# Context columns from the host's layout, and one value product in each of eight steps, in a Flamingo block

## The chip, the cores and the metric

The kernel runs as one program on one core of a Trainium2 chip. The metric is the device time of one execution in microseconds (us). The kernel before took 1677.72, 1670.6 and 1677.48 us in three runs, a median of 1677.48 us. Its profiled execution took 1674.65 us; the profile's span, from the first to the last instruction, is 1672.8 us of it.

## The reference

64 sequences of 128 rows and 256 columns pass through a gated cross attention and a quantised feed-forward layer. Cut to what matters:

```python
# attention: 16 heads of 64, one context sequence for each sequence of x
q = layernorm(x) @ Wq;  k = ctx @ Wk;  v = ctx @ Wv          # (64, 128, 1024)
dots = einsum('bhid,bhjd->bhij', q, k) / 8                    # causal and key mask
out  = einsum('bhij,bhjd->bhid', softmax(dots), v)
x = x + tanh(g_xattn) * (out @ Wo + bo)
# feed-forward: 16-bit fake quantisation of the activations after every step,
# 4-bit weights with one scale for 32 values (lpbq_dequant)
x = x + tanh(g_ffn) * ffn(layernorm(x), w_gate, w_up, w_down)
```

`lpbq_dequant` divides each block of 32 weights by its largest magnitude over 7, rounds, and multiplies back.

## The kernel before

The program is a chain of stages. The first, `attention` (L76), makes the attention and the second layernorm; four more make the gate products, the up products, the maxima and the down products of the feed-forward layer. The change touches the first stage and the queue of data for it.

**Tiling.** Sequences go in 16 groups of 4 (NB = 4, 512 tokens). A group has 8 steps; step c makes heads 2c and 2c+1 (128 of the 1024 inner columns). Unit u = 8g + c is one such pair of heads in one group. The first and the last group are written out, and the 14 between them are one loop. The text counts groups from 0 to 15 and steps from 0 to 7.

**One step on TensorE (`step`, L929).** Every fp32 product is three passes of rounded halves (high by high, low by high, high by low) for each of two 128-row parts of the contraction. In order: the q product of unit u (6 matmuls of 512 columns, into one of two PSUM banks `proj`), the k product (6), the output product of unit u-4 (12 of 256 columns, into `y`), the value products of this step (6 each), probabilities times values of unit u-3 into `pv` (`times_v`), and the scores of unit u.

**Banks.** All products that go through `proj` are a list of jobs; job i writes bank i mod 2 and waits (`copied`) until the job two places before it in the list is copied out. So a value product shares its bank with the q product of its step, and waits for ScalarE's copy `qT` (L509).

**The values** of a group are 8 products (4 sequences by 2 halves of 512 columns). `V_AT` spreads them: two in step 0, one in each of steps 1 to 6, none in step 7. VectorE copies those of steps 0 to 2 out (L661), ScalarE those of steps 3 to 6 (L528). Heads of the first half are first used by `times_v` in step 3, those of the second half in step 7.

**The inputs of the next group.** x and the context are loaded with rows on partitions, and TensorE turns them (`transpose_in`, L857) through `proj` in step 7: two jobs of four 128x128 transposes for x, two for the context. For each job ScalarE copies the rounded high half (`tx_hi`, `tc_hi`, L476), and VectorE subtracts it for the low half (`tx_lo`, `tc_lo`, L617).

**Around TensorE.** ScalarE's order in a step: `qT`, four exponentials of unit u-1 for one head, `kT` (L498), four for the other, the rounded probabilities `prob_parts` of the first head (L491), the value copy, the high half of the output `o_hi` (L532), `prob_parts` of the second head. VectorE's: mask and maximum of the first head (L636, L638), `o_lo` for unit u-4 (L643), `probT` (L624), mask and maximum of the second head, reciprocals (L630), and pieces of the layernorms that the step number chooses (`residual`, which reads `y`, in step 3). GpSimd scales the probabilities (L422), makes their low half (L427) and one `probT` (L434), the reciprocal roots of the layernorms (L412 in step 3), and `xres` in step 6 (L448). SP's queue turns the fp16 halves of the probabilities by DMA and loads the inputs.

**Feed-forward weights.** They are loaded with one wait in unit 3 (`load_ffn`), and VectorE dequantises them in group 0 and group 15 (table `beside`, L738): maximum, scale and reciprocal (`weight_scales`), integers (`weight_ints`), values (`weight_values`), always at the end of the step that the table names. The halves of Wo are made at the end of steps 0 to 2 of group 0 (`w_low_part`).

Of the kernel before, what the change touches and what calls it, by code (L numbers as in the profile page):

```python
# [29 lines left out]
P = 128  # L30
NB = 4
# [44 lines left out]
def attention(nc, x, ctx, mask, g_xattn, wq, wk, wv, wo, bo, w_ffn, ident, ones, x1_d, xn2_d, w_raw, amax_x, wd, hand):  # L76
# [14 lines left out]
    V_AT = [[0, 1], [2], [3]] + [[NB + n] for n in range(NB)] + [[]]  # L91
# [4 lines left out]
    jobs += [(NC - 1, "t", n) for n in range(2 * KC)]  # L96
    NJ = len(jobs)
    FIRST = 2 * KC
# [13 lines left out]
    with ExitStack() as st:  # L112
# [11 lines left out]
        ctx_in = sb("ctx_in", [P, NB, D])  # L124
# [65 lines left out]
        high_done = sem("high_done")  # L190
        scored = sem("scored")
# [10 lines left out]
        transposed = sem("transposed")  # L202
# [10 lines left out]
        half_out = sem("half_out")  # L213
# [73 lines left out]
        def _(sp):  # L287
            def load_ctx(g):
                sp.dma_start(ctx_in[:], ctx[bass.ds(g * NB, NB)].rearrange("b p d -> p b d")).then_inc(ctx_loaded, 16)
# [58 lines left out]
            def load_ffn():  # L348
                sp.wait_ge(w_ready, len(PIECES))
                for n, w in enumerate(w_ffn):  # L350
# [9 lines left out]
            for u in range(U):  # L360
# [8 lines left out]
                if u == 3:  # L369
                    load_ffn()  # L370
# [96 lines left out]
        def _(act):  # L467
# [4 lines left out]
            def high(g, i, n):  # L472

                b, before = nth(g, i)
                act.wait_ge(projected[b], before + 1)
                nc.scalar.activation(t_hi[n // KC][:, n % KC, :], proj[b][:], ACT.Copy).then_inc(high_done, 1)  # L476
# [23 lines left out]
            def step(g, c):  # L500
# [23 lines left out]
                if new and c > 2:  # L524
                    for i, n in jobs_of(c, "v"):
                        b, before = nth(g, i)
                        act.wait_ge(projected[b], before + 1)
                        nc.scalar.activation(v_sb[:, n % NB, VH:2 * VH], proj[b][:], ACT.Copy).then_inc(copied[b], 1)  # L528
# [4 lines left out]
                if nxt:  # L533
                    high(g, *ts[3])
                if soft:
                    high_prob(u - 1, 1, c % 2, NC // 2 * g + c // 2)
                if isinstance(g, int) and g == 0 and c < 3:
                    w_high_part(4 + c)
# [3 lines left out]
            for n in range(2 * KC):  # L542
                high(-1, first_job(n), n)
            w_high_part(2)
# [19 lines left out]
            act.wait_ge(transposed, 1)  # L564
# [10 lines left out]
        def _(dve):  # L575
# [37 lines left out]
            def low(g, i, n, high_before):  # L613
# [3 lines left out]
                nc.vector.tensor_tensor(t_lo[n // KC][:, n % KC, :], proj[b][:], t_hi[n // KC][:, n % KC, :].bitcast(F32),  # L617
                                        ALU.subtract).then_inc(copied[b], 1)

# [37 lines left out]
            def values(g, c):  # L657
                for i, n in jobs_of(c, "v"):
                    b, before = nth(g, i)
                    dve.wait_ge(projected[b], before + 1)  # L660
                    nc.vector.tensor_copy(v_sb[:, n % NB, 0:VH], proj[b][:]).then_inc(copied[b], 1)  # L661

            def step(g, c):
# [33 lines left out]
                if c < 3:  # L697
# [7 lines left out]
                if nxt:  # L705
                    for n in range(2, 4):
                        low(g, *ts[n], 2 * KC * (g + 1) + n)
                if isinstance(g, int):
                    for work, n in beside.get((g, c), []):
                        work(n)  # L710
# [9 lines left out]
            def weight_scales(n):  # L720
                dve.wait_ge(ffn_loaded, 48)
                wait(dve, dequantised, 5 * n)
                nc.vector.tensor_reduce(w_max[:], blocks(n), X, ALU.max, apply_absolute_value=True).then_inc(dequantised, 1)
                dve.wait_ge(dequantised, 5 * n + 1)
# [1511 lines left out]
```

## Time and profile before

| | us |
|---|---|
| median of three runs | 1677.48 |
| profiled execution | 1674.65 |
| its span | 1672.8 |
| TensorE matmuls busy | 1558.6 (93%), weight loads 1270.2 (76%) |
| VectorE busy | 1376.2 (82%) |
| ScalarE busy | 1254.1 (75%) |
| GpSimd busy | 1022.8 (61%) |

The span falls into the start (to 13.69 us, where the first q product begins), group 0 (to 91.12), groups 1 to 14 (to 1010.85), group 15 (to 1084.72), the tail of the attention (to about 1110), and the feed-forward stages. Matmuls are pipelined: a busy row of TensorE counts an instruction from its start to its end, though the next has started. How long a part of a step lasts is read from start to start.

### The profile page before, as it was taken

The numbers are of one execution on the slowest core, as the hardware profiler recorded it, in microseconds if no ns is written. First come the engines' busy times: TensorE is split into PE (matmuls) and PEld (weight loads), VectorE is DVE, ScalarE is ACT, GpSimd is POOL, SyncE is SP. The second block draws the span as 40 slices with busy tenths as digits, with TensorE's granted clock in tenths as the row PEclk, the third lists the DMA queues.
The fourth block names the chain that finished last, engine by engine and source line by source line (L and its number), as shares of the span: only waits on it lengthen the run. The fifth ranks groups of instructions, "written<-read, shape, count | busy, mean of one in ns | idle before, by whom it ended". The sixth has DMA issues, their size and how long they took to land. (4 is left out here: it accounts for less than half of the span.)

```text
span 1672.8 us, 38339 instructions
## 1 busy us (share of the span) xinstructions
PE 1558.6 (93%) x12684; PEld 1270.2 (76%) x12684; DVE 1376.2 (82%) x2243; ACT 1254.1 (75%) x3238; POOL 1022.8 (61%) x1004
## 2 busy tenths in 40 slices
PE   7799999999999999999999998889997997995998
PEld 5687877877878778778778786667775776774887
DVE  6778878878888778888788887768887998998997
ACT  5677878778777778787777776747666998985665
POOL 3878878878779788788788796800004665560000
PEclk9999999999999999999999999989998999997999
DMA  5535444544444454445444442439986885664664
GB/s 172 131 78 127 95 101 104 119 101 101 110 106 100 89 126 96 101 104 118 102 101 112 104 100 55 98 118 327 335 286 219 279 282 188 239 245 171 220 220 149
DMA packets 351460, 252.22 MB, mean 151 GB/s; under 512 B 287792, under 2 KB 325808, under 8 KB 348464
## 3 DMA queue, kind: packets, MB, share of 16 engines
q1 hardware_dynamic: 351408, 251.58, 53.3%
q8 instruction: 26, 0.43, 0.1%
q14 instruction: 26, 0.21, 0.0%
HBM read 105.25 MB, written 76.02 MB: 108 GB/s over the span
## 5 line engine op out<-in xcount | busy, mean ns | idle before, releaser
L483 ACT ACTIVATE prob<-masked,neg_max 128x128 f32<-128x128 f32 x1024 | 397.5, 391 | 67.5 <-DVE neg_max L638 65.4
L427 POOL TENSOR_TENSOR prob_parts<-prob,prob_parts 128x512 f16<-128x512 f32 x254 | 299.3, 1197 | 4.2 <-ACT prob_parts L491 2.4
L422 POOL TENSOR_TENSOR prob<-prob,scaled 128x512 f32<-128x512 f32 x256 | 269.8, 1054 | 20.0
L636 DVE TENSOR_TENSOR masked<-score,mask_add 128x512 f32<-128x512 f32 x256 | 174.8, 683 | 70.6 <-PE score L912 70.6
L491 ACT ACTIVATE prob_parts<-prob 128x512 f16<-128x512 f32 x254 | 159.4, 628 | 55.3 <-POOL prob L422 54.0
L483 ACT ACTIVATION_READ_ACCUMULATOR prob<-masked,neg_max 128x1 f32 x1024 | 193.3, 189 | 0.0
L638 DVE TENSOR_REDUCE neg_max<-masked 128x4 f32<-128x512 f32 x256 | 175.6, 686 | 8.8
L434 POOL TENSOR_TENSOR probT<-turn 128x512 f32<-128x512 f16 x125 | 177.7, 1421 | 0.0
L420 POOL TENSOR_TENSOR scaled<-rsums,pscale 128x4 f32<-128x4 f32 x256 | 58.8, 230 | 181.7 <-DVE rsums L630 181.4
L925 PE MATMUL y<-wo_hi,o_hi 128*128 128x256 f32 x508 | 150.3, 296 | 20.1 <-DVE o_lo L643 19.5
L1676 POOL TENSOR_SCALAR xThi<-n_x 128x1024 fp32r<-128x1024 int16 x15 | 44.7, 2981 | 202.4 <-DMA n_x<-n_x_d 166.6
L509 ACT ACTIVATE qT<-proj 128x512 f32<-128x512 f32 x128 | 76.5, 598 | 96.6 <-PE proj L840 96.6
L898 PEld LDWEIGHTS pv<-probT,v_sb 128*64 128x64 f32 x2048 | 110.2, 138 | 46.7 <-issue 43.3
L898 PE MATMUL pv<-probT,v_sb 128*64 128x128 f32 x2048 | 141.6, 281 | 3.7 <-DVE probT L624 2.8
L925 PE MATMUL y<-wo_lo,o_hi 128*128 128x256 f32 x508 | 144.9, 285 | 0.0
L925 PE MATMUL y<-wo_hi,o_lo 128*128 128x256 f32 x508 | 144.6, 285 | 0.0
L1037 PE MATMUL pair<-xThi,wup_hi 128*128 128x512 f32 x312 | 125.0, 401 | 15.6 <-PEq L1397 5.8
L2106 PE MATMUL y<-wd_both,h_hi 128*128 128x512 f32 x384 | 134.6, 394 | 4.7 <-ACT h_lo L2005 4.7
L925 PEld LDWEIGHTS y<-wo_hi,o_hi 128*128 128x128 f32 x508 | 97.3, 191 | 37.4 <-DVE o_lo L643 34.4
L624 DVE TENSOR_TENSOR probT<-turn 128x512 f32<-128x512 f16 x129 | 123.4, 958 | 0.0
L1037 PE MATMUL pair<-xThi,wup_lo 128*128 128x512 f32 x312 | 123.4, 396 | 0.0
L1037 PE MATMUL pair<-xTlo,wup_hi 128*128 128x512 f32 x312 | 123.4, 395 | 0.0
(251 smaller groups left out, 4526.6 us busy)
## 6 DMA issues: line engine op xcount, KB each, us to landing
gate<-gate_d SPq DMA_DIRECT2D x30, 768.0 KB, 4.3
n_x<-n_x_d SPq DMA_DIRECT2D x25, 512.0 KB, 5.1
gate_d<-stage SPq DMA_DIRECT2D x8, 1536.0 KB, 5.5
n_u_d<-w_raw SPq DMA_DIRECT2D x16, 768.0 KB, 4.1
stage<-n_u_d SPq DMA_DIRECT2D x16, 768.0 KB, 6.2
gate_d<-gate SPq DMA_DIRECT2D x7, 1536.0 KB, 5.5
x_in<-in_x SPq DMA_DIRECT2D x16, 512.0 KB, 4.1
ctx_in<-in_ctx SPq DMA_DIRECT2D x16, 512.0 KB, 4.9
```

The lines of the kernel that those rows point to most:

```text
L422: gp.tensor_tensor(prob[:, h], prob[:, h], scaled[:, h, :].rearrange("p (b o) -> p b o", o=1).broadcast_to([P, NB, P]), ALU.mult).then_inc ...
L427: gp.tensor_tensor(prob_parts[:, h, 1], prob[:, h].rearrange("p b k -> p (b k)"), prob_parts[:, h, 0], ALU.subtract).then_inc(prob_low, 1)
L434: gp.tensor_tensor(probT[:, 1], turn[:, slot, 1, 0:NB], turn[:, slot, 1, NB:2 * NB], ALU.add).then_inc(probT_copied[1], 1)
L483: nc.scalar.activation(prob[:, h, b, :], masked[:, h, b, :], ACT.Exp, bias=neg_max[:, h, b:b + 1], accum_out=psums[:, h, b:b + 1]).then_in ...
L491: nc.scalar.activation(prob_parts[:, h, 0], prob[:, h].rearrange("p b k -> p (b k)"), ACT.Copy).then_inc(prob_high, 1)
L624: nc.vector.tensor_tensor(probT[:, h], turn[:, slot, h, 0:NB], turn[:, slot, h, NB:2 * NB], ALU.add).then_inc(probT_copied[h], 1)
L636: nc.vector.tensor_tensor(masked[:, h], score[h][:], mask_add[:], ALU.add).then_inc(masked_done, 1)
L638: nc.vector.tensor_reduce(neg_max[:, h, :], masked[:, h], X, ALU.max, negate=True).then_inc(max_done, 1)
L898: last = nc.tensor.matmul(pv[h * HD:(h + 1) * HD, b, :], v_sb[:, b, c * P + h * HD:c * P + (h + 1) * HD], probT[:, h, b, :], start=True, s ...
L925: last = nc.tensor.matmul(y[:, e, :], o[s][:, e * P:(e + 1) * P], w[m][:, c * D:(c + 1) * D], start=(c == 0 and j == 0 and e % 2 == 0), st ...
L1037: last = nc.tensor.matmul(bank, stat(s, k), mov(m, k), start=(j == 0), stop=(j == len(passes) - 1))
L2106: nc.tensor.matmul(y[b][:, e], h_hi[:, h, cols], wd[:, :, at:at + D], start=(h == 0 and j == 0), stop=(h == 1 and j == HJ - 1), skip_group ...
```

## The change

1. The host hands the context over as columns: `ctx_columns` has 256 rows and 8192 tokens. The kernel loads 256 by 512 of it into `ctx_in`. The two transposing jobs of the context, their two copies on ScalarE and two subtractions on VectorE go. In their place ScalarE rounds the whole tile once (`ctx_high_part`, 128x1024, SBUF to SBUF), and VectorE subtracts once (`ctx_low_part`, 128x1024, both operands in SBUF), after the second x job in step 7. The k product of step 0 waits for it (`ctx_split`); the second half of the q product of step 0 waits for the second x job.
2. `V_AT` has one value product in each step, number n in step n. Those of steps 0, 1, 2 and 7 are copied by VectorE, those of 3 to 6 by ScalarE. TensorE makes the value product right after the k product, in front of the output product. In steps 3 and 7 `times_v` waits for the copy of the value product of the same step.
3. The feed-forward weights are loaded in two parts (down in unit 2, up and gate in unit 4) and dequantised in the order down, gate, up, in smaller pieces and in other steps; some pieces stand in front of the second reciprocals (`between`). The second half of the last weight's values is made in the tail. The low half of Wo is made in two pieces.
4. In group 0 ScalarE rounds the attention weights before the probabilities of the step, not after them.

```diff
-    V_AT = [[0, 1], [2], [3]] + [[NB + n] for n in range(NB)] + [[]]
+    V_AT = [[n] for n in range(NC)]
+    V_DVE = (0, 1, 2, NC - 1)
-    jobs += [(NC - 1, "t", n) for n in range(2 * KC)]
+    jobs += [(NC - 1, "t", n) for n in range(KC)]
...
-                sp.dma_start(ctx_in[:], ctx[bass.ds(g * NB, NB)].rearrange("b p d -> p b d")).then_inc(ctx_loaded, 16)
+                sp.dma_start(ctx_in[:], ctx_t[:, bass.ds(g * T, T)].rearrange("(k p) t -> p k t", p=P)).then_inc(ctx_loaded, 16)
...
-                columns_made(g - 1, 2 * KC - 1)
+                sp.wait_ge(ctx_split, g)
                 load_ctx(g)
...
-                if u == 3:
-                    load_ffn()
+                if u == 2:
+                    load_ffn(5, (2,))
+                if u == 4:
+                    sp.wait_ge(ffn_loaded, 16)
+                    load_ffn(len(PIECES), (0, 1))
...
+            def ctx_high_part(g):
+                act.wait_ge(ctx_loaded, 16 * (g + 1))
+                if not (isinstance(g, int) and g == 0):
+                    (i, _), = jobs_of(NC - 1, "k")
+                    b, before = nth(g - 1, i)
+                    act.wait_ge(projected[b], before + 1)
+                nc.scalar.activation(t_hi[1][:], ctx_in[:], ACT.Copy).then_inc(high_done, 1)
...
                 if soft:
                     exps(u - 1, 0)
-                if nxt:
-                    high(g, *ts[0])
                 if new:
                     copy_k(g, c, u)
                 if nxt:
-                    high(g, *ts[1])
+                    high(g, *ts[0])
                 if soft:
                     exps(u - 1, 1)
                 if nxt:
-                    high(g, *ts[2])
+                    high(g, *ts[1])
+                    ctx_high_part(g + 1)
+                if isinstance(g, int) and g == 0 and c < 3:
+                    w_high_part(4 + c)
                 if soft:
                     high_prob(u - 1, 0, c % 2, NC // 2 * g + c // 2)
-                if new and c > 2:
+                if new and c not in V_DVE:
...
+            def ctx_low_part(g):
+                dve.wait_ge(high_done, (KC + 1) * (g + 1))
+                nc.vector.tensor_tensor(t_lo[1][:], ctx_in[:], t_hi[1][:].bitcast(F32), ALU.subtract).then_inc(ctx_split, 1)
...
+                if c == NC - 1:
+                    values(g, c)
                 if nxt:
-                    for n in range(2):
-                        low(g, *ts[n], 2 * KC * (g + 1) + n)
+                    low(g, *ts[0], (KC + 1) * (g + 1))
+                if isinstance(g, int):
+                    for work, args in between.get((g, c), []):
+                        work(*args)
                 if soft:
                     reciprocals(u - 1, 1)
...
                 if nxt:
-                    for n in range(2, 4):
-                        low(g, *ts[n], 2 * KC * (g + 1) + n)
+                    low(g, *ts[1], (KC + 1) * (g + 1) + 1)
+                    ctx_low_part(g + 1)
...
+            between = {(0, 3): [(w_low_half, (6, 1))],
+                       (0, 4): [(weight_scales, (0,))],
+                       (0, 5): [(weight_values, (0, 0))],
+                       (G - 1, 1): [(weight_max, (1,))],
+                       (G - 1, 2): [(weight_ints, (1,))],
+                       (G - 1, 6): [(weight_max, (2,))],
+                       (G - 1, 7): [(weight_ints, (2,))]}
+            beside = {(0, 0): [(w_low_part, (4,))],
+                      (0, 1): [(w_low_part, (5,))],
+                      (0, 2): [(w_low_half, (6, 0))],
+                      (0, 3): [(weight_max, (0,))],
+                      (0, 4): [(weight_ints, (0,))],
+                      (0, 5): [(weight_values, (0, 1))],
+                      (G - 1, 1): [(weight_scales, (1,))],
+                      (G - 1, 3): [(weight_values, (1, 0))],
+                      (G - 1, 5): [(weight_values, (1, 1))],
+                      (G - 1, 6): [(weight_scales, (2,))]}
...
+                def part_split(k):
+                    if n == 1 and k == 0:
+                        pe.wait_ge(ctx_split, g + 1)
+                    if n == 0 and k == 1:
+                        (j, _), = jobs_of(c, "k")
+                        pe.wait_ge(copied[j % 2], nth(g, j)[1])
...
+                if new:
+                    for i, n in jobs_of(c, "v"):
+                        value(g, i, n)
                 if nxt:
                     transpose_in(g, *ts[0])
                 if oldest:
...
                     out_product(u - 4, (c - 4) % NC)
                 if nxt:
                     transpose_in(g, *ts[1])
-                if first or fourth:
-                    pe.wait_ge(w_ready, 3 if first else 6)
+                if old and c in (3, NC - 1):
+                    (i, _), = jobs_of(c, "v")
+                    b, before = nth(g, i)
+                    pe.wait_ge(copied[b], before + 1)
+                if old:
+                    times_v(u - 3, co, (g, c, u) if new else None)
```

## Rows read from the trace of the kernel before

**Rows 1.** Stretches: engines' busy time, then granted clock, DMA share, GB/s.
```profile
13.69:91.12 77.43, 62.02 (x544) 48.91 (x544) 55.55 (x86) 50.64 (x159) 48.41 (x49) 0.91 0.44 112
91.12:1010.85 919.73, 898.71 (x8961) 729.57 (x8961) 747.00 (x1498) 719.91 (x2465) 762.44 (x827) 1.00 0.46 105
1010.85:1084.72 73.87, 64.92 (x624) 52.61 (x624) 57.43 (x98) 49.77 (x174) 54.90 (x59) 0.95 0.37 80
...
1110.00:1672.80 562.80, 504.99 (x2332) 413.64 (x2332) 490.99 (x502) 419.37 (x407) 147.56 (x50) 0.95 0.70 240
```

**Rows 2.** Waits of TensorE from 0 to 1110 us: total, times, longest.
```profile
PE y L925 <- DVE o_lo L643: 19.5, 21, 3.4
PE proj L840 <- DVE tc_lo L617: 8.9, 16, 1.0
...
PE proj L840 <- ACT v_sb L528: 4.6, 15, 1.3
```

**Rows 3.** Timeline of TensorE, step 3 of group 8: start, duration, instruction.
```profile
575.92 0.50 PE L840 MATMUL proj<-tx_hi,wq_hi 128*128 128x512 f32 x1
...
580.22 0.40 PE L840 MATMUL proj<-wv_hi,tc_hi 128*128 128x512 f32 x1
...
581.70 1.09 PE L898 MATMUL pv<-probT,v_sb 128*64 128x128 f32 x16
...
583.55 0.50 PE L840 MATMUL proj<-tx_hi,wq_hi 128*128 128x512 f32 x1
```

**Rows 4.** Timeline of ScalarE, the value copy of that step.
```profile
582.79 0.58 ACT L528 ACTIVATE v_sb<-proj 128x512 f32<-128x512 f32 x1
```

**Rows 5.** Timeline of TensorE, step 7 of group 8 and step 0 of group 9.
```profile
606.74 0.50 PE L840 MATMUL proj<-tx_hi,wq_hi 128*128 128x512 f32 x1
...
608.63 0.50 PE L840 MATMUL proj<-tc_hi,wk_hi 128*128 128x512 f32 x1 [0.23 <-ACT v_sb L528]
...
612.62 0.65 PE L869 MATMUL proj<-ident,x_in 128*128 128x128 f32 x4 [0.40 <-ACT kT L498]
...
614.68 0.66 PE L869 MATMUL proj<-ident,ctx_in 128*128 128x128 f32 x4
...
616.70 0.50 PE L840 MATMUL proj<-tx_hi,wq_hi 128*128 128x512 f32 x1 [0.53 <-DVE tc_lo L617]
...
626.35 0.50 PE L840 MATMUL proj<-tx_hi,wq_hi 128*128 128x512 f32 x1
```

**Rows 6.** Timeline of ScalarE, the same step 7.
```profile
609.47 0.60 ACT L509 ACTIVATE qT<-proj 128x512 f32<-128x512 f32 x1
...
611.50 0.58 ACT L476 ACTIVATE tx_hi<-proj 128x512 fp32r<-128x512 f32 x1
...
614.95 0.39 ACT L483 ACTIVATE prob<-masked,neg_max 128x128 f32<-128x128 f32 x1
```

**Rows 7.** Timeline of GpSimd, the same step 7.
```profile
616.00 1.04 POOL L422 TENSOR_TENSOR prob<-prob,scaled 128x512 f32<-128x512 f32 x1
617.00 2.29 POOL L427 TENSOR_TENSOR prob_parts<-prob,prob_parts 128x512 f16<-128x512 f32 x2
```

**Rows 8.** Timelines: rounding and subtracting 128x1024 of a weight in SBUF.
```profile
13.25 1.05 ACT L470 ACTIVATE wv_hi<-v_sb 128x1024 fp32r<-128x1024 f32 x1
...
14.34 1.23 DVE L578 TENSOR_TENSOR wv_lo<-v_sb,wv_hi 128x1024 fp32r<-128x1024 f32 x1 [0.19 <-ACT wv_hi L470]
...
30.86 1.67 DVE L578 TENSOR_TENSOR wv_lo<-v_sb,wv_hi 128x1024 fp32r<-128x1024 f32 x1 [2.47 <-ACT wv_hi L470]
```

**Rows 9.** Timeline of TensorE, two long waits for `o_lo`, in groups 0 and 15.
```profile
84.12 0.58 PE L925 MATMUL y<-wo_hi,o_hi 128*128 128x256 f32 x1 [3.09 <-DVE o_lo L643]
...
1048.16 0.39 PE L925 MATMUL y<-wo_hi,o_hi 128*128 128x256 f32 x1 [3.11 <-DVE o_lo L643]
```

**Rows 10.** Stretches of the granted clock (the column before the DMA share) behind these waits.
```profile
84.30:87.50 3.20, 3.20 (x16) 3.20 (x17) 2.31 (x5) 1.80 (x7) 1.24 (x2) 0.52 0.00 0
...
1046.80:1050.20 3.40, 2.04 (x15) 1.96 (x16) 3.35 (x7) 2.27 (x10) 0.41 (x2) 1.00 0.32 53
```

More of the change, by code:

```diff
@@ L73, in __init__, with attention @@
         self.x_transposed = sem("x_transposed")
-def attention(nc, x, ctx, mask, g_xattn, wq, wk, wv, wo, bo, w_ffn, ident, ones, x1_d, xn2_d, w_raw, amax_x, wd, hand):
+def attention(nc, x, ctx_t, mask, g_xattn, wq, wk, wv, wo, bo, w_ffn, ident, ones, x1_d, xn2_d, w_raw, amax_x, wd, hand):
     B, S, D = x.shape
@@ L346, in load_xres, with load_ffn @@
                 sp.dma_start(xres[:], x[bass.ds(g * NB, NB)].rearrange("b p d -> p b d")).then_inc(xres_loaded, 16)
[L348 to L350 removed]
+            def load_ffn(ready, weights):
+                sp.wait_ge(w_ready, ready)
+                for n in weights:
+                    w = w_ffn[n]
                     sp.dma_start(w_raw[:, n * W1:(n + 1) * W1].rearrange("p (c n) -> p c n", n=w.shape[1]),
@@ new lines, in weight_values @@
+            def weight_values(m, half):
+                dve.wait_ge(dequantised, 5 * m + 4)
+                rows = slice(half * NBLK // 2, (half + 1) * NBLK // 2)
+                last = nc.vector.tensor_tensor(blocks(ORDER[m])[:, rows], ints[:, rows], wide(w_scale)[:, rows], ALU.mult)
+                if half == 1:
+                    last.then_inc(dequantised, 1)
+            between = {(0, 3): [(w_low_half, (6, 1))],
[5 more added lines that the diff above has]
+                       (G - 1, 7): [(weight_ints, (2,))]}
@@ L784, in _ @@
             w_low_part(1)
-            for n in range(2 * KC):
+            for n in range(KC):
                 low(-1, first_job(n), n, n)
+            ctx_low_part(0)
             w_low_part(2)
@@ L833, in _, with product @@
             pe.wait_ge(consts, 1)
-            def product(b, before, stat, mov, n=KC):
+            def product(b, before, stat, mov, new_part=None):
                 wait(pe, copied[b], before)
-                passes = [(k, s, m) for k in range(n) for s, m in split(0, 1)]
+                passes = [(k, s, m) for k in range(KC) for s, m in split(0, 1)]
                 for j, (k, s, m) in enumerate(passes):
+                    if new_part is not None and (s, m) == (0, 0):
+                        new_part(k)
                     last = nc.tensor.matmul(proj[b][:], stat(s, k), mov(m, k), start=(j == 0), stop=(j == len(passes) - 1))
@@ L955, in step @@
                     transpose_in(g, *ts[1])
-                if first or fourth:
-                    pe.wait_ge(w_ready, 3 if first else 6)
-                if new:
-                    for i, n in jobs_of(c, "v"):
-                        value(g, i, n)
-                if nxt:
-                    transpose_in(g, *ts[2])
-                if old:
-                    times_v(u - 3, co, (g, c, u) if new and not nxt else None)
-                if nxt:
-                    transpose_in(g, *ts[3], (g, c, u))
-                if new:
-                    if not (nxt or old):
+                if old and c in (3, NC - 1):
[4 more added lines that the diff above has]
+                    times_v(u - 3, co, (g, c, u) if new else None)
+                if new:
+                    if not old:
                         scores_free(g, c, u)
@@ L973, in _ @@
                 nc.tensor.transpose(trans[:, n % NB, :], ident[:], ident[:])
-            for n in range(2 * KC):
+            for n in range(KC):
                 transpose_in(-1, first_job(n), n)
@@ L2160, in program @@
         hand = Handover(nc, before_n_p, G, D, KC, IC)
-        attention(nc, x, ctx, mask, g_xattn, wq, wk, wv, wo, bo, (w_up, w_gate, w_down), ident, ones, x1_d, xn2_d, w_raw, amax_x, wd, hand)
+        attention(nc, x, ctx_t, mask, g_xattn, wq, wk, wv, wo, bo, (w_up, w_gate, w_down), ident, ones, x1_d, xn2_d, w_raw, amax_x, wd, hand)
         gate = sb("gate", [P, N])
```

107 lines of the change are left out of this document (52 added, 55 removed).

## The prediction, made before the result was known

> **What bounds the kernel now.** I read the busy line first, then the span cut into stages, TensorE's waits, and the timeline of one group. The stages: groups 1 to 14 take 919.73 us, with matmuls on TensorE for 898.71 of them at a granted clock of 1.00; groups 0 and 15 take 77.43 and 73.87 us for the same eight steps at 0.91 and 0.95 [rows 1]. A group in the loop is 919.73 / 14 = 65.7 us. The feed-forward part (562.80 us) isn't touched. So three things count: the group in the loop, fourteen times; the two irregular groups; what TensorE waits for.
>
> A step in the middle of a group is full of matmuls: from 575.92 to 583.55, 7.63 us, with a value product of 1.48 us in it (580.22 to 581.70) [rows 3]. Eight of them are 61.0 us, so a group loses 4.7 us elsewhere. The step starts of group 8 and 9 say where: step 7 takes 9.96 us (606.74 to 616.70), step 0 takes 9.65 (616.70 to 626.35) [rows 5], step 5 takes 7.93, the rest 7.63. In steps 7 and 0 stand four transposing jobs of about 0.5 us and two value products instead of one, and waits: for `v_sb`, `kT` and `tc_lo` [rows 5]. The waits of TensorE up to 1110 us are led by `o_lo`, 19.5 us in 21 places, the longest 3.4, then `tc_lo` with 8.9 in 16 [rows 2]. The `o_lo` waits are VectorE being late, the long ones behind pieces of weight work in groups 0 and 15, each about 3.1 [rows 9].
>
> **Steps 7 and 0 in the loop.** I lay the new order over the old starts, in us from the start of step 7 (606.74). The q product is unchanged, the k product starts at 1.89, when ScalarE has copied the value product of step 6 [rows 5]; GpSimd's `xres` is behind that, and it stays. The value product follows at 3.38: its bank needs `qT`, which ends at 609.47 + 0.60, or 3.33 [rows 6]. It ends at 4.80. The first x job needs `kT`. ScalarE now makes `kT` where `tx_hi` stood, at 611.50 or 4.76 [rows 6], so the job starts at 5.40, 0.6 after TensorE is free. It takes 0.41, the output product 1.43, the second x job 0.49, `pv` 1.05, the scores 0.83 (the same parts from start to start in the old step): step 7 ends at 9.61, against 9.96.
>
> In step 0 the q product ends at 11.1 and the k product then waits for the context split. From the last exponential of the second head (old: 614.95) ScalarE needs 0.87 for it and the second x copy, and 1.05 for the new rounding [rows 6, 8]; VectorE starts the subtraction 1.95 after that exponential starts. The new exponential starts at about 7.73, so the subtraction starts at 9.68, takes 1.23 [rows 8], and ends at 10.9 to 11.0: just in time. After that nothing in step 0 waits. The output product starts 4.3 after the start of the step instead of 3.4, while `o_lo` is ready 3.4 after it. Step 0 becomes 7.63 like the others. Together 17.24 against 19.61: 2.37 saved. Step 5 loses its small `o_lo` wait: 0.30 saved.
>
> **The wait that the change adds in step 3.** `times_v` of step 3 now needs the value product of step 3, and ScalarE copies it at 582.79 to 583.37 [rows 4], 7.45 after the start of the step; it stands behind eight exponentials and the rounded probabilities, which wait for GpSimd (the layernorm root is in front of its scaling in this step). The product itself moves 1.4 earlier, the copy does not, since it isn't the product that it waits for. `pv` started at 581.70, 5.78 in [rows 3]; now at 7.50. That is 1.72 us of TensorE standing still in each group. The copy lies at 7.42 to 7.45 in all 14 groups. Queued behind it on ScalarE are `o_hi` and the second `prob_parts`; behind `pv` are the scores, and so the masks of step 4: all move with TensorE and cost nothing more. VectorE's `residual` in the same step waits for the output product, now 1.4 later, inside that gap. In step 7 the same wait is on VectorE's copy, ready near 5.8 against `pv` at 7.73: nothing.
>
> Sum for a group: 2.37 + 0.30 - 1.72 = 0.95 saved; times 14 = 13.3 us. The transposes and products removed from the busy time are worth more (about 2 times 0.5 us of jobs); most of the rest of the 4.7 us was waiting, and 1.7 of waiting comes back in another step.
>
> **Group 0 and the start.** The first q product starts at 13.69 [rows 1]; before it, two x jobs and two context jobs go through two banks with their copies, and only the context pair is dropped: 2.2 us earlier. Steps 0 to 3 are led by the attention weights (rounded by ScalarE, subtracted by VectorE); I lay them out in the new order and get step 3 at about 32.4 (was 37.6). There the new wait bites harder: the copy of that value product stands behind exponentials that wait for the mask and maximum, which wait for the first half of Wo's low part. `pv` starts at about 43.4 (was 46.66), 5 us after TensorE is free, at the lower clock. Step 4 starts 3.3 us earlier than before. Steps 4 to 7 took 7.65, 12.16, 7.62 and 13.56. The 12.16 and the 13.56 are a wait for `o_lo` of 2.9 and 3.09 [rows 9] and a stretch at the lower clock behind it, 3.20 us at 0.52 [rows 10]. In pieces, and with `o_lo` needed 1.4 later, they become about 7.7 and 9.7: 8.4 saved. Together 11.7. Bounds: 8 (step 4 no earlier than before, the rest gone), and 14 (no loss in step 3).
>
> **Group 15.** 73.87 us [rows 1]. Step 1 took 13.90 (`o_lo` 3.35 late, then 6.6 us at the lower clock), step 3 10.99 (3.11 late [rows 9], clock unchanged [rows 10]), step 7 8.82. The pieces now are the maximum in step 1 (about 1.7), integers in step 2 (2.2) and halves of the values (0.9), all behind the output product's need. I take 7.63 for steps 0 to 2 and 4 to 6, 10.0 for step 3 (its copy comes later still, VectorE being loaded), 8.1 for step 7 with its value product: 63.9, or 10.0 saved. Bounds: 6 and 11.5.
>
> **The tail.** Half of the last weight's values (0.9) now stands between the last-but-one `o_lo` and the copy of `probT` that the last `pv` needs; TensorE has the output product for most of it: +0.3, between 0 and +1.5. Loads: the same 512 KB a group, in runs of 2 KB instead of 1 KB, issued a whole group ahead; nothing either way. SP now waits for the split, done 1.4 into step 0, before it loads the next context; behind that wait stand the probability transposes, and it used to reach this point 4.2 into step 0: nothing.
>
> **The clock.** All of groups 1 to 14 ran at 1.00 [rows 1]. A wait of 3.09 was followed by 0.52, one of 3.11 by 1.00 [rows 9, 10]; waits up to 1.4 never lowered it, one of 2.13 in the tail did. The new wait of 1.72 lies between. A fall costs half of some 3.2 us, 1.6 us. From none of the 16 to all 16 groups that is 0 to 26 us. Nearest to it are waits of 1.4 (no fall) and 2.1 (fall), so I take a fall in one group of ten or so: +2.
>
> **The sum.** -13.3 - 11.7 - 10.0 + 0.3 + 2 = -32.7 us. The profiled execution of 1674.65 becomes 1642; it lies 2.8 below the median of the three runs, and the timed value is then 1677.5 - 32.7 = 1644.8, or 1642 if it is near the profiled one. I say 1643.
>
> **Rivals.**
> *A, the context split is late.* VectorE's subtraction has both operands in SBUF. The same instruction took 1.23 when GpSimd was idle and 1.67 when GpSimd was in an operation (29.18 to 31.46) at its start [rows 8]. In step 7 GpSimd scales for 1.04 and goes on to two subtractions of 1.16 (616.00, 617.00) [rows 7], 1.05 and 2.05 after the last exponential; VectorE arrives at 1.95. If it gets its turn at 2.09, it is in time; if the next GpSimd operation is in first, it starts 1.1 later, and the k product of step 0 waits 1.05, fifteen times: +16, so 1659. For it: a margin of 0.1 us. Against: two neighbouring cases where VectorE, arriving in one GpSimd operation, ran before the next.
> The Trainium skill (SBUF — State Buffer, section "SBUF: two separate sides") says that a VectorE operation with two SBUF inputs and a GpSimd operation that reads SBUF exclude each other for the whole instruction, and that the first to start holds the ports. By that rule the case turns on which starts first, and it would give this rival's time if GpSimd is.
>
> *B, the clock falls behind the new wait in nearly every group.* +26 - 2 = +24: 1667. For: the wait is longer than any in the loop now. Against: it is below every wait that was followed by a fall.
>
> *C, the wait in step 3 outweighs the rest: slower.* The mechanism is that of step 3, ScalarE's copy behind GpSimd. It must cost 32.7 / 16 = 2.0 us a group more than my 1.72. That happens if the gap brings a fall of the clock that lasts two stretches (3.2 us) in each group: +51 - 2, so 1692; it decides from 2.0 a group. Against: after `pv` everything is dense again, and single falls lasted one stretch in five of six cases in the attention.
>
> *D, the pieces still delay TensorE in groups 0 and 15*, as before: VectorE is 72 and 78% busy there [rows 1]. Then only the loop and the start pay: 13.3 + 3, so 1661.
>
> **Chances.** Forecast 0.55 (own range 1634 to 1652), A 0.2, B 0.08, C 0.04, D 0.13. Range for 8 in 10: 1633 to 1664. A measurement of this kernel tells 0.5%, 8.4 us, from no change. Faster by more: the forecast, A, D and half of B, 0.9; within 0.5%: 0.06; slower: 0.04.
>
> **What would show it.** In the changed kernel's loop: a `pv` in step 3 with about 1.7 us idle before it, released by ScalarE's `v_sb`; step 3 of 9.35, step 7 of 9.6, step 0 of 7.63 (8.7 if A), step 5 of 7.63, group about 64.7. No `o_lo` wait over 1 us in groups 0 and 15 apart from the tail. A longer `pv` wait in step 3 of groups 0 (about 5) and 15 (about 2.4). The clock of groups 1 to 14 at 0.97 or more. I am wrong if `pv` in step 3 waits for nothing, if value products wait for `qT`, or if step 0 still takes 9 us.

## The result, and the profile after

| | before | after |
|---|---|---|
| median (11 runs each) | 1675.62 us | 1667.36 us |
| lowest to highest | 1670.6 to 1678.67 | 1663.54 to 1669.37 |
| profiled execution, its span | 1674.65, 1672.8 | 1667.13, 1665.3 |

The ratio is 0.9951, 95% interval 0.9939 to 0.9963: 8 us faster, clear of the noise, where 33 were forecast, and outside the range of 1633 to 1664.

The same stretches as [rows 1] in the kernel after (the granted clock is the column before the DMA share). Group 0 begins at 11.61 us, group 1 at 82.49, group 15 at 1013.27; the last row is the rest of the span:

```profile
11.61:82.49 70.88, 58.46 (x537) 45.73 (x537) 55.01 (x89) 50.99 (x159) 47.86 (x49) 0.93 0.51 135
82.49:1013.27 930.78, 885.11 (x8852) 741.73 (x8849) 768.59 (x1485) 719.07 (x2451) 776.77 (x827) 0.99 0.45 104
1013.27:1079.80 66.53, 63.23 (x628) 52.85 (x624) 57.14 (x98) 49.20 (x172) 56.67 (x57) 0.97 0.41 88
1079.80:1665.30 585.50, 523.38 (x2500) 430.00 (x2496) 511.15 (x541) 429.83 (x437) 156.56 (x60) 0.96 0.68 234
```

Start and group 0 gained 8.6 us, group 15 gained 7.3, what follows 2.6 (588.1 before). Groups 1 to 14 became 11.05 us slower, 930.78 against 919.73, though TensorE has 13.6 us less of matmuls in them: removed work turned into waiting. Waits of TensorE from 0 to 1110 us (total, times, longest), against [rows 2]:

```profile
PE pv L952 <- ACT v_sb L543: 37.3, 16, 5.6
PE proj L890 <- ACT v_sb L543: 12.5, 16, 1.0
PE proj L923 <- ACT kT L512: 5.5, 15, 0.5
...
PE y L979 <- DVE o_lo L669: 3.3, 2, 2.2
```

`o_lo` fell from 19.5 to 3.3 and `tc_lo` is gone; in their place `pv` waits 37.3 us for ScalarE's copy of the values, once in each group, in step 3. The step lengths of groups 1 to 14 (start of a q product to the next, mean):

| step | 0 | 1, 2 | 3 | 4 | 5 | 6 | 7 | group |
|---|---|---|---|---|---|---|---|---|
| before | 9.66 | 7.63 | 7.63 | 7.63 | 7.93 | 7.63 | 9.97 | 65.7 |
| forecast | 7.63 | 7.63 | 9.35 | 7.63 | 7.63 | 7.63 | 9.61 | 64.75 |
| after | 7.60 | 7.61 | 10.14 | 8.04 | 7.61 | 7.62 | 10.27 | 66.5 |

Step 3 of group 8 on TensorE, against [rows 3], and ScalarE's copy in it, against [rows 4]:

```profile
571.26 0.50 PE L890 MATMUL proj<-tx_hi,wq_hi 128*128 128x512 f32 x1
...
579.22 1.09 PE L952 MATMUL pv<-probT,v_sb 128*64 128x128 f32 x16 [2.13 <-ACT v_sb L543]
...
581.08 0.50 PE L890 MATMUL proj<-tx_hi,wq_hi 128*128 128x512 f32 x1
```

```profile
578.59 0.58 ACT L543 ACTIVATE v_sb<-proj 128x512 f32<-128x512 f32 x1
```

The copy ends 7.91 us into the step, not 7.45, and `pv` starts at 7.96 instead of 5.78: 2.2 us of waiting. The wait of step 3 is counted here from start to start, as the forecast did: how much later `pv` starts than it would with no wait. That gives 2.19 as the mean of the loop; the idle time in brackets, from the modelled end of the last matmul, is smaller (2.09 to 2.13). Why the copy is later stands two engines up. VectorE's `probT` of this step in the kernel after, and GpSimd's work beside it:

```profile
573.42 1.30 DVE L650 TENSOR_TENSOR probT<-turn 128x512 f32<-128x512 f16 x1
...
575.35 0.69 DVE L664 TENSOR_REDUCE neg_max<-masked 128x4 f32<-128x512 f32 x1
```

```profile
571.87 2.30 POOL L432 TENSOR_TENSOR prob_parts<-prob,prob_parts 128x512 f16<-128x512 f32 x2
```

The same two in the kernel before, for step 3 from 575.92:

```profile
578.08 0.83 DVE L624 TENSOR_TENSOR probT<-turn 128x512 f32<-128x512 f16 x1
```

```profile
576.07 2.30 POOL L427 TENSOR_TENSOR prob_parts<-prob,prob_parts 128x512 f16<-128x512 f32 x2
```

GpSimd's `prob_parts` of the step before starts 0.61 us into step 3, where it started 0.15 in; `probT`, which ends 0.55 after the end of it in both kernels, takes 1.30 instead of 0.83; the maximum, the exponentials and the copy are 0.46 later. So GpSimd's lag behind TensorE is what to follow. It stands for a ring of three engines: GpSimd's scaling waits in turn for VectorE's reciprocals (0.4 to 0.5 us idle in front of it in these steps of the kernel after), and these for ScalarE's exponentials; which of the three leads isn't shown. The end of GpSimd's last `prob_parts` of a step, after the end of that step on TensorE, in group 8:

| step | 0 | 1 | 2 | 3 | 4 |
|---|---|---|---|---|---|
| before | 1.72 | 2.65 | 2.45 | 2.23 | 2.20 |
| after | 3.27 | 3.09 | 2.91 | 1.65 | 2.62 |

At the end of step 7 the lag is 2.60 before and 3.36 after: the long step 0 of before brings it down to 1.72, the short one of after only to 3.27. Of the 1.55 between them 0.44 is left after step 1 (in the kernel before, GpSimd then stands idle 2.04 us for VectorE's reciprocals; in the kernel after 0.46), and it no longer shrinks: 0.46 after step 2.

The clock: first the stretch of step 3 of group 1 up to `pv`, the wait in it, then the stretches behind the same wait in groups 1 and 2 of the kernel after:

```profile
105.30:113.40 8.10, 5.98 (x36) 5.03 (x34) 6.03 (x10) 6.11 (x22) 7.16 (x9) 1.00 0.39 68
114.60:117.90 3.30, 3.30 (x38) 2.74 (x31) 1.88 (x3) 0.90 (x2) 2.94 (x3) 0.54 0.41 79
...
181.50:184.80 3.30, 3.30 (x44) 2.76 (x37) 2.43 (x4) 1.93 (x6) 3.00 (x3) 1.00 0.41 78
```

After the same wait the clock fell to its lower level (1.2 GHz) in groups 1, 3, 5, 7, 10, 12 and 14, and stayed at the upper in the others. Groups with a fall took some 67.1 us, those without 65.9: in steps 3 and 4 together 18.96 against 17.40, in step 7 10.08 against 10.46.

Step 7 of group 8, against [rows 5]:

```profile
603.93 0.50 PE L890 MATMUL proj<-tx_hi,wq_hi 128*128 128x512 f32 x1
...
606.58 0.50 PE L890 MATMUL proj<-tc_hi,wk_hi 128*128 128x512 f32 x1 [0.98 <-ACT v_sb L543]
...
610.08 0.66 PE L923 MATMUL proj<-ident,x_in 128*128 128x128 f32 x4 [0.37 <-ACT kT L512]
...
614.39 0.50 PE L890 MATMUL proj<-tx_hi,wq_hi 128*128 128x512 f32 x1
...
621.99 0.50 PE L890 MATMUL proj<-tx_hi,wq_hi 128*128 128x512 f32 x1
```

The k product starts 2.65 into the step, not 1.89. The bank it needs is freed by the value copy of step 6, behind GpSimd's `xres`, which started 5.25 into step 6 (4.49 before):

```profile
601.55 2.37 POOL L453 TENSOR_TENSOR xres<-xres,bo_g 128x1024 f32<-128x1024 f32 x1
```

```profile
605.41 0.63 ACT L505 ACTIVATE prob_parts<-prob 128x512 f16<-128x512 f32 x1 [2.75 <-POOL prob L427]
605.94 0.58 ACT L543 ACTIVATE v_sb<-proj 128x512 f32<-128x512 f32 x1
```

Step 0 is 7.60: the context split was in time. VectorE was first at it, and GpSimd's pair of subtractions, which started inside it at 614.93, took 2.82 us where the same pair took 2.30 in step 2. The k product started at 615.88, 0.29 after the split had ended:

```profile
614.36 1.23 DVE L634 TENSOR_TENSOR tc_lo<-ctx_in,tc_hi 128x1024 fp32r<-128x1024 f32 x1 [0.26 <-ACT tc_hi L490]
```

### The profile page after: what moved, and what is told of

It reads as the page before. It is cut to its first block and busy times, and to the rows that moved or that the text cites. A ratio compares the mean times of both kernels' runs of the same rounds, so it can differ in the third digit from the quotient of the medians.

```text
span 1665.3 us, 38115 instructions
## 1 busy us (share of the span) xinstructions
PE 1537.8 (92%) x12556; PEld 1277.5 (77%) x12556; DVE 1397.8 (84%) x2231; ACT 1252.7 (75%) x3222; POOL 1040.9 (63%) x1004
## 5 line engine op out<-in xcount | busy, mean ns | idle before, releaser
L432 POOL TENSOR_TENSOR prob_parts<-prob,prob_parts 128x512 f16<-128x512 f32 x254 | 314.2, 1256 | 14.4 <-ACT prob_parts L505 14.4
L952 PE MATMUL pv<-probT,v_sb 128*64 128x128 f32 x2048 | 142.7, 282 | 37.4 <-ACT v_sb L543 37.3
L425 POOL TENSOR_TENSOR scaled<-rsums,pscale 128x4 f32<-128x4 f32 x256 | 65.2, 255 | 149.2 <-DVE rsums L656 149.2
L979 PE MATMUL y<-wo_hi,o_hi 128*128 128x256 f32 x508 | 145.1, 286 | 3.3 <-DVE o_lo L669 3.3
L650 DVE TENSOR_TENSOR probT<-turn 128x512 f32<-128x512 f16 x129 | 144.5, 1121 | 0.0
L966 PE MATMUL score<-kT,qT 64*64 64x128 f32 (+1 forms) x4096 | 120.5, 257 | 2.3 <-ACT kT L512 1.8
```

The source lines that it names most:

```text
L432: gp.tensor_tensor(prob_parts[:, h, 1], prob[:, h].rearrange("p b k -> p (b k)"), prob_parts[:, h, 0], ALU.subtract).then_inc(prob_low, 1)
L650: nc.vector.tensor_tensor(probT[:, h], turn[:, slot, h, 0:NB], turn[:, slot, h, NB:2 * NB], ALU.add).then_inc(probT_copied[h], 1)
L952: last = nc.tensor.matmul(pv[h * HD:(h + 1) * HD, b, :], v_sb[:, b, c * P + h * HD:c * P + (h + 1) * HD], probT[:, h, b, :], start=True, s ...
L979: last = nc.tensor.matmul(y[:, e, :], o[s][:, e * P:(e + 1) * P], w[m][:, c * D:(c + 1) * D], start=(c == 0 and j == 0 and e % 2 == 0), st ...
```

## The experiments

Each ratio is against the kernel before, on the same chip, with its 95% interval. "Loop" is groups 1 to 14: 919.73 us before, 930.78 after.

**The parts of the change.** First, the kernel before with only parts 3 and 4 (the weights):

```diff
 kernel before
+load_ffn in two parts; tables between and beside, w_low_half, weight_* as in the change
```

> The kernel before, with only the weights' part of the change: loads in two parts, the new order and pieces of the dequantisation, Wo's low half in two, ScalarE's rounding of the attention weights before the probabilities. Theory (the parts add up; groups 0 and 15 gained from the pieces, the loop lost from the value products): groups 1 to 14 stay at 919.7 us; group 0 ends 6 to 9 us earlier, group 15 is 6 to 8 us shorter: about 1660 us, 0.991. Rival (the pieces only help because the output product moved behind the value product): o_lo waits of over 1 us stay in groups 0 and 15, and the gain is under 6 us.

Measured: 1655.62 us, 0.988 (0.9856 to 0.9905), loop 919.70. The theory held, with more gained than the 13 to 17 us expected: parts 3 and 4 are worth 21 us, 11.6 in group 0 (65.81) and 9.7 in group 15 (64.2). The longest `o_lo` wait of group 15 ahead of its step 7 is 0.26.

```diff
 kernel after
-    V_AT = [[n] for n in range(NC)]
+    V_AT = [[0, 1], [2], [3]] + [[NB + n] for n in range(NB)] + [[]]
...  (value products behind the output product, no wait for v_sb in steps 3 and 7)
```

> The changed kernel with the value products where they were before: two in step 0, one in steps 1 to 6, none in step 7, behind the output product, copied as before, and no wait in steps 3 and 7. Context columns and weight pieces stay. Theory (the value products' new places are the loss): step 3 is 7.6, step 5 about 7.9, step 7 about 8.6 to 9, step 0 about 9.3 to 9.6; a group is about 64.2, the loop 899 instead of 930.8; about 1635 us, 0.976. Rival (without the slack that the context jobs gave, GpSimd falls behind and waits come back wherever the values stand): a group stays at 65.5 or more: over 1655 us.

Measured: 1634.61, 0.9748 (0.9726 to 0.977), loop 900.65, with steps 0 and 7 of 10.42 and 7.84 and no step above 7.94 between them. So parts 1, 3 and 4 are worth 42 us, and part 2, the new order of the value products, costs 33. By difference, part 1 is worth 21; it was not run alone.

**The copy in step 3.** ScalarE copies the value product of step 3 right behind `kT`:

```diff
                 if new:
                     copy_k(g, c, u)
+                if new and c in V_EARLY:          # V_EARLY = (3,)
+                    (the value copy)
...
-                if new and c not in V_DVE:
+                if new and c not in V_DVE and c not in V_EARLY:
```

> The changed kernel, with one move: in step 3 ScalarE copies the value product right after kT, in front of the second head's exponentials. Theory (the wait in step 3 comes from the copy's place in ScalarE's order, and the clock falls come from that wait): pv in step 3 waits under 0.3 us instead of 2.19, groups 1 to 14 run at a clock of 1.00, step 3 is 7.6 to 7.8 and step 4 7.6 in every group; step 7 stays at 10.0 to 10.5. A group goes from 66.5 to about 63.8 us, 37 us over the loop, and 5 to 8 more in groups 0 and 15: about 1625 us, 0.97 of before. Rival (GpSimd is what is late, and the copy's place only shows it): the wait comes back elsewhere in steps 4 to 7, a group stays above 65.5 us: over 1655 us.

Measured: 1621.35, 0.9666 (0.9641 to 0.9691), loop 889.06. `pv` in step 3 of group 8 waits for nothing, 5.75 into the step:

```profile
545.46 0.50 PE L896 MATMUL proj<-tx_hi,wq_hi 128*128 128x512 f32 x1
...
551.21 1.09 PE L958 MATMUL pv<-probT,v_sb 128*64 128x128 f32 x16
```

```profile
78.08:967.14 889.06, 873.13 (x8852) 733.74 (x8849) 764.84 (x1485) 716.39 (x2451) 781.52 (x827) 1.00 0.48 109
```

Steps 3 and 4 take 7.60 and 7.61, no clock falls in the loop, group 0 ends 4.4 us earlier (`pv` in its step 3 still waits 2.05 of idle time) and group 15's steps 3 and 4 fall from 11.42 and 8.53 to 8.68 and 7.96. One move of one copy is worth 46 us: the place of the wait is shown. GpSimd is not less late here, 2.88 us after step 2 and 3.94 after step 3, but in steps 3 to 6 TensorE no longer waits for what hangs on it.

**GpSimd's root out of the way**, a smaller cut of the same wait:

```diff
-                if c == 3 and new and more:
-                    make_rstd(g + 1)
...
+                if c == 3 and new and more:       # at the end of the step
+                    make_rstd(g + 1)
```

> The changed kernel, with GpSimd's reciprocal root of step 3 (1.02 us) moved from in front of the scaling of the probabilities to the end of its step. Theory of ScalarE's order: the copy is behind eight exponentials that end 0.3 us before it is released, so the wait of pv shrinks from 2.19 to about 1.9 and the clock falls a little less often: 1660 to 1665 us. Rival (GpSimd's lateness sets the wait): the wait shrinks by about 1.0 to 1.2 us, the falls of the clock end, 1640 us.

Measured: 1647.13, 0.9828 (0.9806 to 0.985), loop 910.94: 20 us where some 5 were expected. The wait shrank from 2.19 to 1.74 (idle 1.65 to 1.69), a little more than to the 1.9 expected; what was missed is that at 1.74 the clock never fell in 14 groups. Step 3 took 9.35, step 4 7.60, and step 7 10.08, its k product being less late too.

**The clock by itself.** TensorE makes 14 transposes of the identity, which nobody reads, in front of the wait in step 3:

```diff
+                if old and c == 3:
+                    for n in range(14):
+                        nc.tensor.transpose(trans[:, n % NB, :], ident[:], ident[:])
                 if old and c in (3, NC - 1):
```

> The changed kernel with 14 transposes of the identity, about 1.6 us of useless TensorE work into an unused bank, in front of the wait of step 3. The output is the same. Theory (a 2.2 us wait is what lets the granted clock fall in half of the groups): the wait for the copy ends at the same time, so step 3 stays at about 9.8 with only 0.6 us of it idle; the clock is 1.00 in all of groups 1 to 14, step 4 is 7.6 in all of them, the loop goes from 930.8 to about 922: about 1657 us. Rival (the falls have another cause, or cost nothing because the next step has room): the loop stays at 930, 1667 us.

Measured: 1662.54, 0.9903 (0.9878 to 0.9929), loop 922.96; some 922 for the loop and 1657 in all were expected. What stands behind group 15, where the code is that of the kernel after, took 3.9 us longer in this execution (589.4 for 585.5). In group 8:

```profile
571.89 1.69 PE L1017 MATMUL trans<-ident 128*128 128x128 f32 x14
...
574.17 1.09 PE L952 MATMUL pv<-probT,v_sb 128*64 128x128 f32 x16 [0.59 <-ACT v_sb L543]
```

`pv` starts 7.94 in, as without the transposes, and all 14 steps 3 take 9.79 to 9.82 and all steps 4 7.60 to 7.62: no clock falls. The falls cost the loop 7.8 us net, not the 2 of the forecast. Net, since step 7 gives part back: it takes 10.46 in every group here, where groups with a fall had 10.05 to 10.10.

**The slack.** If GpSimd's catching up in the long steps 7 and 0 is what the new order took away, putting time back into step 0 must make the wait of step 3 shorter. 18 transposes of the identity stand behind the value product of step 0:

```diff
+                if c == 0 and new and not first:
+                    for n in range(18):
+                        nc.tensor.transpose(trans[:, n % NB, :], ident[:], ident[:])
```

> The changed kernel with 18 transposes of the identity (about 2.1 us of useless TensorE work) behind the value product of step 0 in groups 1 to 15. The output is the same. Theory (the long step 0 of before let GpSimd and VectorE catch up; with it short they stay about 0.5 to 0.8 us later against TensorE, and that is why the waits of steps 3 and 7 came out longer than I worked out from the old starts): step 0 is 9.7, the wait of pv in step 3 falls from 2.19 to about 1.75, the clock falls end, step 7 falls from 10.27 to 9.6 to 9.8: a group about 66.5 as now, 1665 us, within 5 of the changed kernel. Rival (the order of the copy alone makes 2.19): the waits stay, each group gains 2.1 us: about 1697 us.

Measured: 1688.92, 1.006 (1.004 to 1.0079), loop 944.80. The total was missed by 24 us: I had expected all of the added time to come back. The mechanism held for step 3 and failed for step 7. Step 0 takes 9.57 in place of 7.60; GpSimd then ends 1.72, 2.67 and 2.48 us after steps 0, 1 and 2, the lags of the kernel before to 0.03; VectorE's `probT` of step 3 is back to 0.86 (0.83 before, 1.30 after); and `pv` starts 7.53 into step 3, a wait of 1.77 (idle 1.70), near the 1.72 of the forecast:

```profile
583.67 0.86 DVE L650 TENSOR_TENSOR probT<-turn 128x512 f32<-128x512 f16 x1
```

```profile
589.03 1.09 PE L952 MATMUL pv<-probT,v_sb 128*64 128x128 f32 x16 [1.70 <-ACT v_sb L543]
```

Step 3 is 9.38 and step 4 7.61, with no clock fall: in these two steps 1.2 of the 1.97 us come back. Step 7 stays at 10.49, where 9.6 to 9.8 was expected; GpSimd's lag after steps 4 and 5 is as in the kernel after (2.66 and 4.20), so this slack doesn't reach that far.

**Step 7.** GpSimd's `xres` of step 6 at the end of its step, on top of the early copy:

```diff
-                if c == 6 and new:                # between the scaling of the first head
-                    (xres)
...
+                if c == 6 and new:                # at the end of the step
+                    (xres)
```

> Early copy in step 3 as in e1_copy_first, and GpSimd's xres of step 6 (2.4 us) moved from in front of the scaling to the end of the step. Theory (step 7's k product waits 0.8 to 1.1 for the value copy of step 6, which waits on ScalarE for probabilities that GpSimd scales behind xres): that wait goes, qT and kT come earlier, step 7 falls from 10.26 to 9.0 to 9.4, a group from 63.5 to about 62.4: about 1606 us. Rival (xres only moves its 2.4 us in front of GpSimd's probT, and pv of step 7 waits instead): step 7 stays at 10 or more, about 1620 us.

Measured: 1617.51, 0.9631 (0.9615 to 0.9647): 4 us better than the early copy alone, not 15. The k product of step 7 waits no more, yet the step is 10.00 (10.26): the wait moved on to the x jobs. VectorE's copy that the second one waits for stands behind a `probT` of 2.09 us beside `xres`.

```profile
578.92 0.66 PE L929 MATMUL proj<-ident,x_in 128*128 128x128 f32 x4 [0.74 <-ACT kT L513]
...
581.35 0.66 PE L929 MATMUL proj<-ident,x_in 128*128 128x128 f32 x4 [0.34 <-DVE v_sb L693]
```

Both moves of GpSimd together:

> e5_first_and_xres_last, and GpSimd's reciprocal root of step 3 at the end of its step as well. Theory (in a loop where TensorE waits only in step 7, GpSimd's order in step 3 costs nothing): as e5_first_and_xres_last within 2 us. Rival (GpSimd's lateness carries from step 3 to step 7): 3 us or more faster.

Measured: 1629.47, 0.9709 (0.9689 to 0.9728), 12 us slower than without the root's move, and missed. On GpSimd and TensorE, step 4 of group 8:

```profile
561.06 1.01 POOL L418 TENSOR_TENSOR rstd<-vare,mhalf 128x4 f32<-128x4 f32 x1
562.05 1.16 POOL L440 TENSOR_TENSOR probT<-turn 128x512 f32<-128x512 f16 x1
```

```profile
563.30 1.09 PE L958 MATMUL pv<-probT,v_sb 128*64 128x128 f32 x16 [0.32 <-issue]
```

The root, put last in step 3, now stands ahead of the `probT` of step 4; `pv` starts as that ends (563.21), and step 4 takes 8.00, and steps 6 and 7 0.17 and 0.27 more. With the step-3 wait in place TensorE came later and step 4 took 7.60, so the root was covered. The same move gained 20 us there and lost 12 here.

Three runs follow the banks of step 7, each on top of the one before, the first on top of the late `xres`. `kT` ahead of the first exponentials:

```diff
+                if nxt:
+                    copy_k(g, c, u)
                 if soft:
                     exps(u - 1, 0)
-                if new:
+                if new and not nxt:
                     copy_k(g, c, u)
```

> Against the kernel with the early copy and the late xres (1617.5 us, step 7 of 10.00): ScalarE copies kT in step 7 in front of the first four exponentials, which wait for the maximum anyway. There the first x job waited 0.74 to 0.9 us for kT (copied 578.29 to 578.86), and the second x job 0.34 for VectorE's value copy (580.63 to 581.29). Theory 1, the banks pass the wait on: the first x job starts 0.9 earlier, but the second still waits until VectorE has copied the value product at 581.29, behind a probT of 2.09 us; step 7 stays at 10.0 and the time at 1617, plus or minus 3. Theory 2, kT alone set the step: step 7 takes 9.1 us, 15 times 0.9 gone, about 1604.

Measured: 1618.45, 0.9653 (0.9624 to 0.9681), step 7 10.01, as the first theory had it. The first x job waits no more, the second waits for VectorE's copy:

```profile
582.38 0.66 PE L931 MATMUL proj<-ident,x_in 128*128 128x128 f32 x4 [1.30 <-DVE v_sb L695]
```

The value copy of step 7 by ScalarE:

```diff
-    V_DVE, V_EARLY = (0, 1, 2, NC - 1), (3,)
+    V_DVE, V_EARLY = (0, 1, 2), (3, NC - 1)
```

> The run before with ScalarE also copying the value product of step 7, behind the first four exponentials, in place of VectorE. Theory 1: the second x job no longer waits, step 7 takes 8.6 us (matmuls of 7.6 and two x jobs of 0.5); but the exponentials of the second head stay where the maximum puts them, the context is rounded behind them and subtracted until about 585.0, and the k product of step 0, now due at 583.9, waits 1.1: 1.4 less 1.1 in 15 places, about 1612 (1605 to 1618). Theory 2, the split of the context is not what comes next: 1597.

Measured: 1618.04, 0.9655 (0.9623 to 0.9687), where 1612 was expected: step 7 8.67, step 0 8.86. The wait went on to the second x subtraction (idle 0.16) and to the split, the place where rival A had it. Its mechanism was another: the subtraction took 1.23 here too, and was late because step 7 was shorter.

```profile
587.36 0.50 PE L896 MATMUL proj<-tc_hi,wk_hi 128*128 128x512 f32 x1 [0.53 <-DVE tc_lo L642]
```

The context rounded and subtracted ahead of the last four exponentials:

```diff
                 if nxt:
                     high(g, *ts[0])
+                    ctx_high_part(g + 1)
                 if soft:
                     exps(u - 1, 1)
                 if nxt:
                     high(g, *ts[1])
-                    ctx_high_part(g + 1)
...  (VectorE: ctx_low_part behind the first x subtraction)
```

> The run before with the context rounded by ScalarE in front of the last four exponentials of step 7, and subtracted by VectorE right behind the first x subtraction. Theory 1: the k product of step 0 waits no more; what may remain is the second x subtraction, 0.4 to 0.9 us for the second half of the q product of step 0. Step 7 and step 0 together 16.2 to 17.1 against 17.6 of the early-copy kernel, so 1597 to 1610. Theory 2, the exponentials of the second head, 0.6 to 1.2 later, push GpSimd's chain, and steps 1 to 3 get waits for probT or o_lo: not faster than the run before it.

Measured: 1608.87, 0.9593 (0.9564 to 0.9622), loop 878.21, steps 7 and 0 of 8.67 and 8.42. It is the fastest version, within the 1597 to 1610 expected. What is left is the second x subtraction:

```profile
579.98 0.50 PE L896 MATMUL proj<-tx_hi,wq_hi 128*128 128x512 f32 x1 [0.50 <-DVE tx_lo L637]
```

## Why the prediction was wrong

The profiled execution changed by -7.5 us where the sum said -32.7. The 25.2 between them, term by term:

- **The loop: forecast -13.3, with +2 for the clock; measured +11.1. This is the step that failed: "The wait that the change adds in step 3", sized at 1.72.** The mechanism was right: the place, the engine, the copy behind GpSimd. The size came from laying the new TensorE order over ScalarE's old starts ("The product itself moves 1.4 earlier, the copy does not"). But the old starts were those of a GpSimd that had steps 0 and 7 of 9.7 and 10 us to catch up in; the same sum shortened step 0 by 2 us and didn't ask who had been using them. The wait is 2.19. Two things show the cause: with step 0 made as long as before, the lags of before and a wait of 1.77 come back; with the copy taken out of the queue, the wait is gone. In the 14 groups the 0.47 is 6.6 us.
- **The clock: forecast +2, measured about +8** in the loop, net of what step 7 gives back (7 falls of some 1.1 us; 7.8 with the wait filled). The forecast weighed 1.72 between 1.4 and 2.13; 2.19 lies beyond the latter. The waits of 1.74 and 1.77, in 28 groups, had no fall: near the size forecast the term was 0 in both runs, and it fails with the size of the wait. Rival B, given 0.08, named this mechanism and 1667; but seven groups fell, not nearly all, and that it came out right in the total is luck: its 24 us stood for what came from the longer wait and from step 7.
- **Step 7: forecast 9.61, measured 10.27, 14 times 0.66 is 9.2 us.** "GpSimd's `xres` is behind that, and it stays" is the same error: it stood 0.76 later, and the k product with it. Each bank then hands its wait on: k, first x job, second x job, context split, second x subtraction, as five runs showed one after the other. The lateness of steps 4 and 5 behind it is shown only in part: the root's move brought `xres` to 4.83 and step 7 to 10.08, more slack in step 0 did not. What makes up the rest stays open. In the loop, the wait is 6.6, the falls cost 10.9 in steps 3 and 4 (7 times 1.56), and step 7, which has what they give back already in its mean, is 9.2; the other steps came out up to 0.03 shorter each, some -1.8. Together 24.9, where the loop missed its -13.3 by 24.4.
- **Step 0: forecast 7.63, measured 7.60.** Right, and rival A (0.2) did not come: the k product didn't wait for the split. The margin was small, as argued, 0.29 for the 0.1 of the forecast, and VectorE did come first; with step 7 shortened from 10.01 to 8.67 the split was late (step 0 8.86).
- **Step 5: 7.63, measured 7.61.** Right.
- **Group 0 and the start: -11.7, measured -8.6,** inside the bounds (8 to 14). Near the lower bound, since step 4 began 1.3 us earlier than before and not 3.3: step 3 began at 34.2 and not at 32.4, and its wait was 5.6 (forecast 5), with the clock at its lower level (0.50) from 42.7 to 49.3, during the wait and behind it. With the copy early, and that wait 2.05, group 0 ends 4.4 us earlier. `o_lo` no longer leads it, as forecast.
- **Group 15: -10.0, measured -7.3,** inside the bounds. The step-3 wait again: step 3 11.42 and step 4 8.53 for 10.0 and 7.63. Rival D is refuted: with the weights alone changed the two groups give 21 us, and the `o_lo` waits are gone from group 15.
- **The tail and after: +0.3, measured -2.6.** The cause of these 3 us stays open, and they may be none of the change's: in four of the runs above whose code is that of the kernel after from there on (the early copy, the late root, the filled wait, the slack) the same stretch took 588.5, 584.4, 589.4 and 589.1 us, a spread of 5.

Rival C needed twice the fall in every group. It was the right question, whether step 3 eats what the rest gives: part 2 costs 33 us and the others give 42. Had the wait been taken at both its ends, at 2.2 with rival B's falls behind it, the upper end would have been 1643 + 6.6 + 24, some 1674, and the range would have held the result.

## What to carry to other kernels

A time laid over old starts holds only for engines whose queue is not late. Before using one, write down how far each following engine lags behind the leader at the end of every step, and where in the period it catches up; if the change shortens that place, every start behind it moves, and each wait sized from them with it. And put a copy that a product of the same step waits for ahead of work that waits for a third engine: here this one line is worth 46 us, more than five times the whole change.

## What the runs showed of the hardware

- The clock fell behind an idle time of 2.09 to 2.13 us in 7 of 14 equal groups, behind 1.65 to 1.71 in none of 28, and in none of 14 when transposes filled 1.69 us of it. This holds for these groups, and is no threshold: in group 0, with other work around, it fell 1.2 us behind an idle time of 1.82 with only the weights changed (0.50 from 43.3 to 46.5), and stayed at 1.00 behind one of 2.05 with the early copy. A fall cost 1.6 us in two steps, and 0.4 of it came back in step 7; that the following engines had caught up in the meantime is a guess.
- VectorE's `probT`, two operands in SBUF, took 0.83 us when it started 0.29 us before the end of GpSimd's instruction, 1.30 when 0.75 was left, and 2.09 when 1.54 was left of `xres` (576.38 to 578.76, in the run with the late `xres`; `probT` started at 577.22). It ended 0.54 to 0.55 after GpSimd's instruction each time; with none of GpSimd's at its start it took 0.68.
